# A fused four-stage image network on one core: half-height transposes for half of each attention block, and the residual one block later

## The chip, the cores and the metric

The kernel runs on one core of one Trainium2 chip. The metric is the device time of one execution in microseconds, from three runs; one further execution was profiled. A core has five engines that run side by side: TensorE (PE in the rows, its weight loads PEld), VectorE (DVE), ScalarE (ACT), GpSimd (POOL) and SyncE (SP), which issues the transfers. Each takes its own instructions in order; between engines they wait for each other by semaphores.

## The reference

Four layers are computed one after the other on an input of 4 batch elements, 32 channels and 96 x 96 pixels, all in float32: halo attention, a deformable convolution, a Fourier layer and an FFT convolution. The change touches the attention alone:

```python
BLOCK, HALO, HEADS = (8, 3, 4)
WIN = BLOCK + 2 * HALO
sim = jnp.einsum('bid,bjd->bij', q, k)      # 64 queries x 196 keys, 8 channels per head
attn = jax.nn.softmax(sim, axis=-1)
out = jnp.einsum('bij,bjd->bid', attn, v)
```

The image is cut into 12 x 12 = 144 blocks of 8 x 8 pixels. The 64 queries of a block look at the 14 x 14 = 196 pixels around it, for 4 heads and 4 batch elements.

## The kernel before

`program` (L2120) calls one stage after the other; `stage_attention` (L138) is the first. After the projections it walks over the 144 blocks (`w` in the code), and each engine has a loop of its own in which `step(w, ...)` does pieces of different blocks. This order is written out by hand, and nothing else sets it.

What is computed for a block, by the helper that does it:

- `keys` and `spread` (GpSimd) add the relative position to the keys of a block and spread its queries over the heads.
- `scores(w, p)` (L428, TensorE): `p` is a pair of batch elements. Four products of 32 rows give the scores, 128 rows (2 heads x 64 queries) x 196 keys each, in the PSUM tile `at_sc` of the pair. There is one such tile per pair.
- `maxes(w, p)` (L356, VectorE): negated row maxima, `at_nmx`.
- `exps(w, p)` (L407, ScalarE): four exponentials into `at_probs`, each with its sum.
- `inverse(w, p)` (L361, VectorE): reciprocals of the sums; `norm(w, p)` (L338, GpSimd) multiplies the probabilities by them.
- `transposed(w, b)` (L440, TensorE): for one batch element, four transposes of 128 queries x 98 keys, into PSUM `at_pt[b % 2]`, so pt0 for the elements 0 and 2 and pt1 for 1 and 3. There are two such tiles in all.
- `evac`: VectorE (L365) copies pt0, ScalarE (L401) copies pt1, to `at_pts`, each twice a block.
- `weigh(w)` (L450, TensorE): eight products of transposed probabilities and values, two halves of the keys (`c`) for four batch elements (`b`), into PSUM `at_ov[w % 2]`.
- `residual(w)` (L371, VectorE): four operations, one per head, that add the result to `x_sb`.

TensorE's step `w` (L463) is: transposes of elements 0 and 1 of block w; scores of pair 0 of block w + 2; `weigh` of block w - 1; transposes of elements 2 and 3 of block w; scores of pair 1 of block w + 2. Each set of four transposes waits for the normalised probabilities and for the copy of the PSUM tile that it writes, from the set before. ScalarE's step (L415) is: exponentials of pair 1 of block w + 1, copy, exponentials of pair 0 of block w + 2, copy. VectorE's step is at L383, GpSimd's at L343. A float32 product is two MATMUL records in the trace, a transpose one.

## Time and profile before

| | us |
|---|---|
| median of three runs | 2141.68 (2127.19 to 2234.55) |
| profiled execution, its time | 2117.36 |
| its span in the trace | 2115.6 |
| busy: PE / DVE / ACT / POOL | 1883.8 / 1280.4 / 1129.5 / 737.5 |
| transposes `at_pt`, 2304 matmuls, busy | 311.3 |
| scores `at_sc`, 2304 matmuls, busy | 272.1 |
| product with the values `at_ov`, 2304 matmuls, busy | 155.0 |
| exponentials and the reading of their sums, ACT, 1152 each, busy | 473.8 and 235.3 |
| copies of `at_pt`, 288 each, busy | DVE 196.2, ACT 171.9 |
| maxima `at_nmx`, DVE, 288, busy | 277.7 |

Times are of one profiled execution. A group is named by its line in the kernel, its engine, and the tile that it writes; "idle" is the time for which the engine did nothing just before an instruction, with the instruction that ended it. Matmuls are pipelined, so their records overlap.

### The profile page before, as it was taken

The page shows a single profiled execution, that of the slowest core. Times are in us where ns is not written, and L with a number is a line of the kernel's source. Part 1 is how long each engine was busy: PE and PEld are TensorE (multiplying, and loading weights), DVE is VectorE, ACT ScalarE, POOL GpSimd, SP SyncE. Part 2 cuts the span into 40 slices and gives each one's busy share as a digit, 9 for nine tenths or more (in the row PEclk, how much of TensorE's full clock was granted, in tenths as well). Part 3 has the DMA queues.
Part 4 walks back from the last instruction along what each step waited for, and adds up shares of the span by engine and source line. Part 5 has one row for each costly group of instructions (what it writes and reads, how often), then busy time and mean ns, then how long its engine had stood idle before and what let it go on. Part 6 is the DMA issues. An engine that isn't in the chain of part 4 may idle for free. (4 is left out here: it accounts for less than half of the span.)

```text
span 2115.6 us, 60272 instructions
## 1 busy us (share of the span) xinstructions
PE 1883.8 (89%) x22133; PEld 1312.7 (62%) x22133; DVE 1280.4 (61%) x2688; ACT 1129.5 (53%) x3617; POOL 737.5 (35%) x671
## 2 busy tenths in 40 slices
PE   5699999999999998279999999768757999999999
PEld 3566666666666666045556655467735777777776
DVE  5178888888888888356788888652462222222222
ACT  2378888888888887266777778400121111111111
POOL 0078787887878876122323333000000000000000
PEclk9889999999999999578999999955778999999999
DMA  4401000000000000565676665250002211121110
GB/s 166 135 19 29 27 28 23 27 28 26 25 26 27 26 25 16 141 164 159 185 186 190 185 191 160 52 98 5 16 15 58 65 46 36 36 62 47 36 36 16
DMA packets 164175, 150.05 MB, mean 71 GB/s; under 512 B 60070, under 2 KB 151340, under 8 KB 163935
## 3 DMA queue, kind: packets, MB, share of 16 engines
q1 hardware_dynamic: 164014, 147.88, 26.3%
q8 instruction: 104, 1.70, 0.3%
q14 instruction: 57, 0.46, 0.1%
HBM read 83.18 MB, written 45.89 MB: 61 GB/s over the span
## 5 line engine op out<-in xcount | busy, mean ns | idle before, releaser
L412 ACT ACTIVATE at_probs<-at_sc,at_nmx 128x196 f32<-128x196 f32 x1152 | 473.8, 424 | 114.1 <-DVE at_nmx L358 114.0
L340 POOL TENSOR_TENSOR at_probs<-at_probs,at_rs 128x784 f32<-128x784 f32 x288 | 430.5, 1495 | 152.6 <-DVE at_rs L363 152.5
L358 DVE TENSOR_REDUCE at_nmx<-at_sc 128x4 f32<-128x784 f32 x288 | 277.7, 964 | 122.3 <-PE at_sc L436 122.3
L447 PE MATMUL at_pt<-at_ident,at_probs 128*98 128x128 f32 x2304 | 311.3, 278 | 40.7 <-DVE at_pts L368 40.1
L447 PEld LDWEIGHTS at_pt<-at_ident,at_probs 128*98 128x98 f32 x2304 | 241.0, 128 | 141.5 <-POOL at_probs L340 78.9
L436 PE MATMUL at_sc<-at_kw,at_qw 32*128 32x196 f32 x2304 | 272.1, 355 | 12.0 <-POOL at_qw L329 8.0
L1247 ACT ACTIVATE dn_mix<-dn_mps 128x432 f32<-128x432 f32 x384 | 182.4, 528 | 119.6 <-PE dn_mps L1142 116.3
L2022 PE MATMUL fc_qps<-fc_wk,fc_xs 99*128 99x128 f32 x1728 | 211.0, 279 | 31.3 <-DMA fc_xs<-in_ones 31.3
L412 ACT ACTIVATION_READ_ACCUMULATOR at_probs<-at_sc,at_nmx 128x1 f32 x1152 | 235.3, 204 | 0.0
L2022 PEld LDWEIGHTS fc_qps<-fc_wk,fc_xs 99*128 99x128 f32 x1728 | 202.1, 194 | 42.0 <-issue 39.1
L436 PEld LDWEIGHTS at_sc<-at_kw,at_qw 32*128 32x128 f32 x2304 | 184.3, 187 | 65.3 <-issue 54.8
L1335 DVE TENSOR_SCALAR dn_mix<-dn_mps 128x432 f32<-128x432 f32 x384 | 213.4, 597 | 18.2 <-PE dn_mps L1142 18.2
L368 DVE COPY at_pts<-at_pt 98x512 f32<-98x512 f32 x288 | 196.2, 681 | 0.8 <-PE at_pt L447 0.8
L1155 PEld LDWEIGHTS dn_sps<-dn_mix,dn_patch 128*32 128x32 f32 x6144 | 142.7, 111 | 76.8 <-issue 59.7
L379 DVE SCALAR_TENSOR_TENSOR x_sb<-at_ov,at_hm,x_sb 128x64 f32 (+1 forms) x576 | 163.5, 284 | 27.7 <-PE at_ov L459 2.8
L1142 PE MATMUL dn_mps<-dn_stack,dn_selw 42*128 42x432 f16 x768 | 177.6, 349 | 1.3 <-DVE dn_mix L1335 0.6
L404 ACT COPY at_pts<-at_pt 98x512 f32<-98x512 f32 x288 | 171.9, 597 | 4.5 <-PE at_pt L447 4.5
L1155 PE MATMUL dn_sps<-dn_mix,dn_patch 128*32 128x96 f32 x6144 | 168.5, 249 | 4.1 <-issue 2.8
L1342 DVE COPY dn_sampled<-dn_sps 128x432 f32<-128x432 f32 x192 | 116.6, 607 | 88.0 <-PE dn_sps L1157 81.2
L1934 ACT COPY fc_vsb<-fc_vps 128x384 f32<-128x384 f32 x48 | 23.0, 479 | 267.1 <-PE fc_vps L2033 267.1
L1928 ACT COPY fc_spec<-fc_fps 128x1024 f32<-128x1024 f32 x72 | 73.0, 1014 | 166.5 <-PE fc_fps L2044 166.5
L459 PE MATMUL at_ov<-at_pts,at_vs 98*32 98x256 f32 x2304 | 155.0, 387 | 1.0 <-DVE at_pts L368 1.0
(154 smaller groups left out, 2309.3 us busy)
## 6 DMA issues: line engine op xcount, KB each, us to landing
fc_xs<-fc_xp SPq DMA_DIRECT2D x144, 120.0 KB
dn_slab<-near_image SPq DMA_DIRECT2D x72, 200.0 KB, 4.3
at_vs<-attention_values SPq DMA_DIRECT2D x288, 49.0 KB
dn_offs<-near_maps SPq DMA_DIRECT2D x24, 486.0 KB
near_corners<-dn_split SPq DMA_DIRECT2D x24, 486.0 KB
dn_stack<-near_corners SPq DMA_DIRECT2D x24, 486.0 KB
dn_patch<-near_pixels SPq DMA_DIRECT2D x24, 384.0 KB
attention_values<-ap_vrow SPq DMA_DIRECT2D x21, 256.0 KB, 2.3
```

Source lines behind the costliest of these rows:

```text
L340: nc.gpsimd.tensor_tensor(probs[s][p][:, :, :, :], probs[s][p][:, :, :, :], rs[s][:, 2 * p:2 * p + 2, :].unsqueeze(3).broadcast_to([P, 2, ...
L358: nc.vector.tensor_reduce(nmx[s][:, 2 * p:2 * p + 2, :], sc[p][:, :, 0:2 * NK].rearrange("p b (j k) -> p b j k", j=2), AX.X, ALU.max, nega ...
L368: nc.vector.tensor_copy(pts[s][b][:, :, :, :], pt[b % 2][0:HK, :].rearrange("p (c j q) -> p c j q", c=2, j=2)).then_inc(even_ready, 1)
L404: nc.scalar.copy(pts[s][b][:, :, :, :], pt[b % 2][0:HK, :].rearrange("p (c j q) -> p c j q", c=2, j=2)).then_inc(odd_ready, 1)
L412: nc.scalar.activation(probs[s][p][:, b, j, :], sc[p][:, b, NK * j:NK * j + NK], ACT.Exp, bias=nmx[s][:, 2 * p + b, j:j + 1], accum_out=su ...
L436: mm = nc.tensor.matmul(sc[p][:, b, NK * j:NK * j + NK], qw[s][r, 2 * j:2 * j + 2, :], kw[s][r, :], start=True, stop=True)
L447: mm = nc.tensor.transpose(pt[b % 2][0:HK, o:o + P], probs[s][p][:, b % 2, j, HK * c:HK * c + HK], ident[:, :])
L1142: nc.tensor.matmul(mps[b][:, 0:COLS], selw[:, :], stack[t % 2][:, b, :, :, 4 * k:4 * k + 4], start=True, stop=True).then_inc(mix_done, 1)
L1155: nc.tensor.matmul(sps[C * g:C * g + C, 2 * PX * b:2 * PX * b + 2 * PX], patch[t % 2][:, k, C * b:C * b + C], fours[:, :, g, :], start=Tru ...
L1247: nc.scalar.activation(mix[s % 2][b][:, :], mps[b][:, 0:COLS], ACT.Relu).then_inc(mix_act, 1)
L1335: nc.vector.tensor_scalar(mix[s % 2][b][:, :], mps[b][:, 0:COLS], 0.0, None, ALU.max).then_inc(mix_dve, 1)
L2022: mm = nc.tensor.matmul(qps[m][:, P * b:P * b + P], rows(i, b, dy * W + P * j, P), wk[:, dy, 0:2 * HID], start=(dy == 0), stop=(dy == 2))
```

## The change

Three things change in `stage_attention`.

The transposes of a block are now made pair by pair. The first pair (`p == 0`) is transposed in eight whole transposes as before. The second pair is transposed in 16 of 64 queries each: rows 0 to 63 go to pt0, rows 64 to 127 to pt1. The copies of the second pair therefore write every other run of 64 in `at_pts`, which has one tile per pair now. `pt_ready` counts pairs.

The waits of the transposes stand in `may_transpose`, for both PSUM tiles and the normalised probabilities. `weigh` is split into its two halves of the keys, one behind each set of scores; `may_transpose` of the transposes that come next is called ahead of the last of the four products of each half.

The residual of a block is added one step later, and there is one more step at the end.

```diff
--- before.py
+++ after.py
@@ -260,7 +260,7 @@
             sums = [sbc(f"sums{i}", [P, B, 2]) for i in range(2)]
             rs = [sbc(f"rs{i}", [P, B, 2]) for i in range(2)]
             probs = [[sbc(f"probs{i}_{p}", [P, 2, 2, NK]) for p in range(2)] for i in range(2)]
-            pts = [[sbc(f"pts{i}_{b}", [HK, 2, 2, P]) for b in range(B)] for i in range(2)]
+            pts = [[sbc(f"pts{i}_{p}", [HK, 2, 2, 2, 2, Q64]) for p in range(2)] for i in range(2)]
             sc = [ctx.enter_context(nc.psum_tensor(f"at_sc{p}", [P, 2, 512], F)) for p in range(2)]
             pt = [ctx.enter_context(nc.psum_tensor(f"at_pt{i}", [P, 512], F)) for i in range(2)]
             ov = [ctx.enter_context(nc.psum_tensor(f"at_ov{i}", [P, 512], F)) for i in range(2)]
@@ -286,6 +286,7 @@
                 for x in range(NROW):
                     step((NROW - 1) * NROW + x, NROW - 1, x)
                 step(NWIN, NROW - 1, NROW)
+                step(NWIN + 1, NROW - 1, NROW + 1)
 
             def corner(gy, x):
 
@@ -362,11 +363,14 @@
                     wait(dve, exp_done, w, 4 * 2, 4 * p + 4)
                     nc.vector.reciprocal(rs[s][:, 2 * p:2 * p + 2, :], sums[s][:, 2 * p:2 * p + 2, :]).then_inc(inv_ready, 1)
 
-                def evac(w, b, s):
-                    wait(dve, pt_ready, w, B, b + 1)
+                def evac(w, p, s):
+                    wait(dve, pt_ready, w, 2, p + 1)
                     wait(dve, pv_done, w, 1, -1)
-                    nc.vector.tensor_copy(pts[s][b][:, :, :, :],
-                                          pt[b % 2][0:HK, :].rearrange("p (c j q) -> p c j q", c=2, j=2)).then_inc(even_ready, 1)
+                    if p == 0:
+                        part = pts[s][p][:, 0, :, :, :, :].rearrange("p c j h q -> p (c j h) q")
+                    else:
+                        part = pts[s][p][:, :, :, :, 0, :].rearrange("p b c j q -> p (b c j) q")
+                    nc.vector.tensor_copy(part, pt[0][0:HK, :].rearrange("p (n q) -> p n q", q=Q64)).then_inc(even_ready, 1)
 
                 def residual(w, gy, x):
                     y0, x0 = corner(gy, x)
@@ -387,10 +391,10 @@
                         maxes(w + 2, 0, x % 2)
                     if there(w + 1):
                         inverse(w + 1, 1, (x + 1) % 2)
-                    if there(w + (-1)):
-                        residual(w + (-1), gy, x - 1)
+                    if there(w + (-2)):
+                        residual(w + (-2), gy, x - 2)
                     if there(w):
-                        evac(w, 2, x % 2)
+                        evac(w, 1, x % 2)
                     if there(w + 2):
                         inverse(w + 2, 0, x % 2)
                         maxes(w + 2, 1, x % 2)
@@ -398,15 +402,18 @@
 
             @block.scalar
             def _(act):
-                def evac(w, b, s):
-                    wait(act, pt_ready, w, B, b + 1)
+                def evac(w, p, s):
+                    wait(act, pt_ready, w, 2, p + 1)
                     wait(act, pv_done, w, 1, -1)
-                    nc.scalar.copy(pts[s][b][:, :, :, :],
-                                   pt[b % 2][0:HK, :].rearrange("p (c j q) -> p c j q", c=2, j=2)).then_inc(odd_ready, 1)
+                    if p == 0:
+                        part = pts[s][p][:, 1, :, :, :, :].rearrange("p c j h q -> p (c j h) q")
+                    else:
+                        part = pts[s][p][:, :, :, :, 1, :].rearrange("p b c j q -> p (b c j) q")
+                    nc.scalar.copy(part, pt[1][0:HK, :].rearrange("p (n q) -> p n q", q=Q64)).then_inc(odd_ready, 1)
 
                 def exps(w, p, s):
                     wait(act, max_ready, w, 2, p + 1)
-                    wait(act, pt_ready, w, B, 2 * p + 2 - 2 * B)
+                    wait(act, pt_ready, w, 2, p + 1 - 2 * 2)
                     for b in range(2):
                         for j in range(2):
                             nc.scalar.activation(probs[s][p][:, b, j, :], sc[p][:, b, NK * j:NK * j + NK], ACT.Exp,
@@ -416,11 +423,11 @@
                     if there(w + 1):
                         exps(w + 1, 1, (x + 1) % 2)
                     if there(w):
-                        evac(w, 1, x % 2)
+                        evac(w, 0, x % 2)
                     if there(w + 2):
                         exps(w + 2, 0, x % 2)
                     if there(w):
-                        evac(w, 3, x % 2)
+                        evac(w, 1, x % 2)
                 rows(act, step)
 
             @block.tensor
@@ -437,43 +444,57 @@
                                                   start=True, stop=True)
                     mm.then_inc(scores_ready, 1)
 
-                def transposed(w, b, s):
-                    p = b // 2
+                def may_transpose(w, p):
                     wait(pe, normed, w, 2, p + 1)
-                    wait(pe, (even_ready, odd_ready)[b % 2], w, 2, p)
-                    for c in range(2):
-                        for j in range(2):
-                            o = (2 * c + j) * P
-                            mm = nc.tensor.transpose(pt[b % 2][0:HK, o:o + P], probs[s][p][:, b % 2, j, HK * c:HK * c + HK], ident[:, :])
+                    wait(pe, even_ready, w, 2, p)
+                    wait(pe, odd_ready, w, 2, p)
+
+                def transposed(w, p, s):
+                    for b in range(2):
+                        for c in range(2):
+                            for j in range(2):
+                                if p == 0:
+                                    o = P * (2 * c + j)
+                                    mm = nc.tensor.transpose(pt[b][0:HK, o:o + P], probs[s][p][:, b, j, HK * c:HK * c + HK], ident[:, :])
+                                for h in range(2 * p):
+                                    o, r = Q64 * (4 * b + 2 * c + j), slice(Q64 * h, Q64 * h + Q64)
+                                    mm = nc.tensor.transpose(pt[h][0:HK, o:o + Q64], probs[s][p][r, b, j, HK * c:HK * c + HK], ident[r, r])
                     mm.then_inc(pt_ready, 1)
 
-                def weigh(w, g, i):
+                def weigh(w, g, i, c, following):
 
                     s = i % 2
-                    wait(pe, even_ready, w, 2, 2)
-                    wait(pe, odd_ready, w, 2, 2)
-                    wait(pe, v_loaded[s], g, 16 * VSRING, 32 * (i // 2 + 1))
-                    wait(pe, res_step, w, HEADS, -HEADS)
-                    for c in range(2):
-                        for b in range(B):
-                            mm = nc.tensor.matmul(ov[s][C * b:C * b + C, 0:256], vs[i % VSRING][:, c, C * b:C * b + C],
-                                                  pts[s][b][:, c, :, :], start=(c == 0), stop=(c == 1))
-                    mm.then_inc(pv_done, 1)
+                    if c == 0:
+                        wait(pe, even_ready, w, 2, 2)
+                        wait(pe, odd_ready, w, 2, 2)
+                        wait(pe, v_loaded[s], g, 16 * VSRING, 32 * (i // 2 + 1))
+                        wait(pe, res_step, w, HEADS, -HEADS)
+                    for b in range(B):
+                        if b == B - 1 and following is not None:
+                            may_transpose(*following)
+                        mm = nc.tensor.matmul(ov[s][C * b:C * b + C, 0:256], vs[i % VSRING][:, c, C * b:C * b + C],
+                                              pts[s][b // 2][:, b % 2, c, :, :, :].rearrange("p j h q -> p (j h q)"), start=(c == 0), stop=(c == 1))
+                    if c == 1:
+                        mm.then_inc(pv_done, 1)
 
                 def step(w, g, i):
                     s = i % 2
                     if there(w):
+                        if not there(w + (-2)):
+                            may_transpose(w, 0)
                         transposed(w, 0, s)
-                        transposed(w, 1, s)
                     if there(w + 2):
                         scores(w + 2, 0, s)
                     if there(w + (-1)):
-                        weigh(w + (-1), g, i - 1)
+                        weigh(w + (-1), g, i - 1, 0, (w, 1) if there(w) else None)
+                    elif there(w):
+                        may_transpose(w, 1)
                     if there(w):
-                        transposed(w, 2, s)
-                        transposed(w, 3, s)
+                        transposed(w, 1, s)
                     if there(w + 2):
                         scores(w + 2, 1, s)
+                    if there(w + (-1)):
+                        weigh(w + (-1), g, i - 1, 1, (w + 1, 0) if there(w + 1) else None)
                 for w in range(-2, 2 * VSRING):
                     step(w, w // VSRING, w % VSRING)
                 with pe.Fori(2, NWIN // VSRING - 1) as g:
```

On TensorE, in the middle of the loop (numbers are of buffers; `at_probs1_0` is the first pair of an odd block): scores of a second pair, transposes of a first pair, scores of the next first pair, and the product with the values. Before:

```order
L436 MATMUL at_sc1<-at_kw0,at_qw0 128x196 [waits at_exp_done]
L436 MATMUL at_sc1<-at_kw0,at_qw0 128x196 x3
L447 MATMUL at_pt0<-at_ident,at_probs1_0 98x128 [waits at_even_ready,at_normed]
L447 MATMUL at_pt0<-at_ident,at_probs1_0 98x128 x3
L447 MATMUL at_pt1<-at_ident,at_probs1_0 98x128 [waits at_odd_ready,at_normed]
L447 MATMUL at_pt1<-at_ident,at_probs1_0 98x128 x3
L436 MATMUL at_sc0<-at_kw1,at_qw1 128x196 [waits at_exp_done,at_keys_ready]
L436 MATMUL at_sc0<-at_kw1,at_qw1 128x196 x3
L459 MATMUL at_ov0<-at_pts0_0,at_vs0 32x256 [waits at_v_loaded0,at_res_step,at_odd_ready,at_even_ready]
L459 MATMUL at_ov0<-at_pts0_1,at_vs0 32x256
L459 MATMUL at_ov0<-at_pts0_2,at_vs0 32x256
L459 MATMUL at_ov0<-at_pts0_3,at_vs0 32x256
```

Now, from the second half of the product with the values on:

```order
L475 MATMUL at_ov1<-at_pts1_0,at_vs3 32x256 x2
L475 MATMUL at_ov1<-at_pts1_1,at_vs3 32x256
L475 MATMUL at_ov1<-at_pts1_1,at_vs3 32x256 [waits at_odd_ready,at_even_ready,at_normed]
L458 MATMUL at_pt0<-at_ident,at_probs1_0 98x128 x4
L458 MATMUL at_pt1<-at_ident,at_probs1_0 98x128 x4
L443 MATMUL at_sc0<-at_kw1,at_qw1 128x196 [waits at_exp_done,at_keys_ready]
L443 MATMUL at_sc0<-at_kw1,at_qw1 128x196 x3
L475 MATMUL at_ov0<-at_pts0_0,at_vs0 32x256 [waits at_v_loaded0,at_res_step,at_odd_ready,at_even_ready]
L475 MATMUL at_ov0<-at_pts0_0,at_vs0 32x256
L475 MATMUL at_ov0<-at_pts0_1,at_vs0 32x256
L475 MATMUL at_ov0<-at_pts0_1,at_vs0 32x256 [waits at_odd_ready,at_even_ready,at_normed]
```

The transposes of a first pair had a wait for each PSUM tile ahead of each four of them; now one wait for both tiles stands ahead of the matmul before them. The product with the values stood in one piece behind the scores of a first pair and now has a half there and a half ahead of the whole transposes.

On ScalarE, one and a half steps at the same place. Before:

```order
L404 COPY at_pts0_1<-at_pt1 98x512 [waits at_pv_done,at_pt_ready]
L412 ACTIVATE at_probs0_0,at_sums0<-at_sc0,at_nmx0 128x196 [waits at_pt_ready,at_max_ready]
L412 ACTIVATE at_probs0_0,at_sums0<-at_sc0,at_nmx0 128x196 x3
L404 COPY at_pts0_3<-at_pt1 98x512 [waits at_pv_done,at_pt_ready]
L412 ACTIVATE at_probs0_1,at_sums0<-at_sc1,at_nmx0 128x196 [waits at_pt_ready,at_max_ready]
L412 ACTIVATE at_probs0_1,at_sums0<-at_sc1,at_nmx0 128x196 x3
L404 COPY at_pts1_1<-at_pt1 98x512 [waits at_pv_done,at_pt_ready]
```

Now:

```order
L412 COPY at_pts0_0<-at_pt1 98x512 [waits at_pv_done,at_pt_ready]
L419 ACTIVATE at_probs0_0,at_sums0<-at_sc0,at_nmx0 128x196 [waits at_pt_ready,at_max_ready]
L419 ACTIVATE at_probs0_0,at_sums0<-at_sc0,at_nmx0 128x196 x3
L412 COPY at_pts0_1<-at_pt1 98x8x64 [waits at_pv_done,at_pt_ready]
L419 ACTIVATE at_probs0_1,at_sums0<-at_sc1,at_nmx0 128x196 [waits at_pt_ready,at_max_ready]
L419 ACTIVATE at_probs0_1,at_sums0<-at_sc1,at_nmx0 128x196 x3
L412 COPY at_pts1_0<-at_pt1 98x512 [waits at_pv_done,at_pt_ready]
```

Nothing moved: a copy of pt1 stands behind each four exponentials, the copy of a second pair (`at_pts0_1`, formerly `at_pts0_3`) behind the exponentials of a first pair. Its shape is 8 runs of 64.

On VectorE, one step. Before:

```order
L368 COPY at_pts1_0<-at_pt0 98x512 [waits at_pv_done,at_pt_ready]
L358 TENSOR_REDUCE at_nmx1<-at_sc0 128x4 [waits at_scores_ready]
L363 RECIPROCAL at_rs0<-at_sums0 128x4 [waits at_exp_done]
L379 SCALAR_TENSOR_TENSOR x_sb<-at_ov0,at_hm,x_sb 128x8x8 [waits at_pv_done]
L379 SCALAR_TENSOR_TENSOR x_sb<-at_ov0,at_hm,x_sb 128x8x8 [waits at_res_step] x3
L368 COPY at_pts1_2<-at_pt0 98x512 [waits at_pv_done,at_pt_ready]
L363 RECIPROCAL at_rs1<-at_sums1 128x4 [waits at_exp_done]
L358 TENSOR_REDUCE at_nmx1<-at_sc1 128x4 [waits at_scores_ready]
```

Now:

```order
L373 COPY at_pts1_0<-at_pt0 98x512 [waits at_pv_done,at_pt_ready]
L359 TENSOR_REDUCE at_nmx1<-at_sc0 128x4 [waits at_scores_ready]
L364 RECIPROCAL at_rs0<-at_sums0 128x4 [waits at_exp_done]
L383 SCALAR_TENSOR_TENSOR x_sb<-at_ov1,at_hm,x_sb 128x8x8 [waits at_pv_done]
L383 SCALAR_TENSOR_TENSOR x_sb<-at_ov1,at_hm,x_sb 128x8x8 [waits at_res_step] x3
L373 COPY at_pts1_1<-at_pt0 98x8x64 [waits at_pv_done,at_pt_ready]
L364 RECIPROCAL at_rs1<-at_sums1 128x4 [waits at_exp_done]
L359 TENSOR_REDUCE at_nmx1<-at_sc1 128x4 [waits at_scores_ready]
```

The order is the same too; the residual reads the other `at_ov` tile, that of the block before.

## Rows read from the trace of the kernel before

**Rows 1.** The page: PE's granted clock in tenths, 40 slices of 52.9 us.
```profile
PEclk9889999999999999578999999955778999999999
```

**Rows 2.** Busy time by stretch: us, busy of each engine, granted clock, DMA.
```profile
400.00:500.00 100.00, 94.02 (x947) 65.42 (x940) 85.69 (x199) 85.71 (x356) 79.79 (x79) 1.00 0.09 27
```

**Rows 3.** Waits, 200 to 800 us: who waited for whom, us, times, longest.
```profile
ACT at_probs L412 <- DVE at_nmx L358: 87.5, 118, 0.8
...
PE at_pt L447 <- DVE at_pts L368: 34.8, 118, 0.3
```

**Rows 4.** Instructions in time order, one block: start, us, engine, line [idle before].
```profile
405.83 1.08 PE L447 MATMUL at_pt<-at_ident,at_probs 128*98 128x128 f32 x8
...
406.03 0.42 ACT L412 ACTIVATE at_probs<-at_sc,at_nmx 128x196 f32<-128x196 f32 x1
406.08 1.24 DVE L379 SCALAR_TENSOR_TENSOR x_sb<-at_ov,at_hm,x_sb 128x64 f32 x4
406.08 1.50 POOL L340 TENSOR_TENSOR at_probs<-at_probs,at_rs 128x784 f32<-128x784 f32 x1 [1.01 <-DVE at_rs L363]
...
406.84 0.93 PE L436 MATMUL at_sc<-at_kw,at_qw 32*128 32x196 f32 x8
...
407.24 0.68 DVE L368 COPY at_pts<-at_pt 98x512 f32<-98x512 f32 x1
...
407.55 0.21 ACT L412 ACTIVATION_READ_ACCUMULATOR at_probs<-at_sc,at_nmx 128x1 f32 x1
407.65 0.60 ACT L404 COPY at_pts<-at_pt 98x512 f32<-98x512 f32 x1
407.84 0.17 DVE L363 RECIPROCAL at_rs<-at_sums 128x4 f32<-128x4 f32 x1
407.92 0.95 DVE L358 TENSOR_REDUCE at_nmx<-at_sc 128x4 f32<-128x784 f32 x1
408.03 0.83 PEld L447 LDWEIGHTS at_pt<-at_ident,at_probs 128*98 128x98 f32 x8 [0.56 <-POOL at_probs L340]
408.06 1.05 PE L447 MATMUL at_pt<-at_ident,at_probs 128*98 128x128 f32 x8 [0.29 <-DVE at_pts L368]
...
408.98 0.42 ACT L412 ACTIVATE at_probs<-at_sc,at_nmx 128x196 f32<-128x196 f32 x1 [0.74 <-DVE at_nmx L358]
...
409.05 0.93 PE L436 MATMUL at_sc<-at_kw,at_qw 32*128 32x196 f32 x8
...
409.91 1.07 PE L459 MATMUL at_ov<-at_pts,at_vs 98*32 98x256 f32 x16
410.03 0.97 DVE L358 TENSOR_REDUCE at_nmx<-at_sc 128x4 f32<-128x784 f32 x1 [0.56 <-PE at_sc L436]
...
410.60 0.59 ACT L404 COPY at_pts<-at_pt 98x512 f32<-98x512 f32 x1
...
410.91 0.53 PE L447 MATMUL at_pt<-at_ident,at_probs 128*98 128x128 f32 x3
...
411.12 0.42 ACT L412 ACTIVATE at_probs<-at_sc,at_nmx 128x196 f32<-128x196 f32 x1
```

**Rows 5.** Records of two lines: count, ns min/median/max, first and last start.
```profile
L447 PE MATMUL at_pt<-at_ident,at_probs x2304: 272/273/450, 109.0 to 841.8; 128*98 128x128 f32 x192
...
L459 PE MATMUL at_ov<-at_pts,at_vs x2304: 379/379/635, 119.5 to 843.7; 98*32 98x256 f32 x192
```

**Rows 6.** In order of time, the last stage, PE and its weight loads.
```profile
1913.55 1.09 PE L2044 MATMUL fc_fps<-fc_qk,fc_dft 64*64 64x256 f32 x16
...
1914.57 0.97 PEld L2055 LDWEIGHTS fc_ips<-fc_dft,fc_prod 128*128 128x128 f32 x8 [0.39 <-issue]
```

**Rows 7.** In order of time, PE near the start of the stage.
```profile
119.45 1.94 PE L459 MATMUL at_ov<-at_pts,at_vs 98*32 98x256 f32 x16
121.32 1.94 PE L447 MATMUL at_pt<-at_ident,at_probs 128*98 128x128 f32 x8
123.19 0.60 PE L436 MATMUL at_sc<-at_kw,at_qw 32*128 32x196 f32 x4
```

## The prediction

> **What bounds the kernel now.** I read the page first, for where attention lies and at which clock; then busy time by stretch; then the waits of 200 to 800 us; and last the instructions of one block of queries in order of time. Attention lies in slices 3 to 16 of 40, at the full clock but for its start [rows 1]. There TensorE (PE) is busy 94.02 of 100 us at a granted clock of 1.00 [rows 2], so it looks like the bound. The waits say otherwise: in every block PE stands still once for VectorE's (DVE) copy of the transposed probabilities, 34.8 us over 118 blocks, and ScalarE (ACT) stands still once for DVE's maxima, 87.5 us [rows 3]. So the block is timed by rings of dependences that close after one block. Names in what follows: T1 and T2 are the transposes of a block's first and second pair, S1 and S2 the score products, O the product with the values, X1 and X2 the four exponentials of a pair, M1 and M2 the maxima, E the DVE copies, A the ACT copies.
>
> The period is 5.09 us: X1 starts at 406.03 and again at 411.12 [rows 4]. The transposes run from 109.0 to 841.8 us, 16 to a block [rows 5], so 144 blocks at 5.1.
>
> Ring 1, PE and DVE, binds today. T1 starts at 408.06, T2 at 410.91 (2.85, with S1 and O between); the residual starts 0.25 after T2 (405.83 to 406.08), since it waits for O; the copy E starts 1.16 after it (407.24); T1 follows 0.82 later, after 0.29 of idle time put down to that copy [rows 4]. 2.85 + 0.25 + 1.16 + 0.82 = 5.08.
>
> Ring 2, ACT and DVE, is just as long. X1 406.03, reciprocal 407.84 (1.81), M2 407.92 (0.08), X2 408.98 (1.06), ACT's copy 410.60 (1.62), next X1 411.12 (0.52): 5.09 [rows 4]. Its only slack is that the reciprocal starts 0.08 after the last read of X1's sums ends (407.55 + 0.21), and some of that is signalling. **So with ring 1 gone the period can fall to 5.01 at the lowest**, and the change leaves every member of ring 2 in its place: in ACT's order a copy stands between the exponentials as before, and on DVE the reciprocal still stands ahead of M2.
>
> **The change part by part.** *Residual a block later.* The same four operations in the same place, but their input is long complete: ring 1 loses its 0.25 and opens. One more residual stands alone at the end: +1 us once.
>
> *Whole transposes of the first pair.* Eight, as before: 1.01 from the first to the next product (405.83 to 406.84). What changes is who must be out of the way. Before, the first four wrote pt0 and waited for DVE alone, the other four wrote pt1 and waited for ACT. Now one wait for both stands ahead of all eight, and one matmul earlier still: before the last of four matmuls of the product with the values, whose split halves stand behind S1 and S2.
>
> *Half transposes of the second pair.* 16 of 64 columns instead of 8 of 128. The trace has no transpose on a row group. Lower bound: products on two row groups do run side by side. The score products, 32 rows each, issue eight in 0.93 [rows 4]; the 64-row products of the last stage issue 16 of 256 columns in 1.09 [rows 6]. A whole transpose takes (1.08 - 0.27) / 7 = 0.115 [rows 4, 5], near 0.11 without the lead-in; a pair of halves would take half of it, 8 x 0.055 = 0.44, and with the lead-in (1.01 - 8 x 0.11 = 0.13) T2 is 0.57. Upper bound: the loads go one by one and set the pace. Loads of 128 columns, with only 64 moving, come every (0.97 - 0.19) / 7 = 0.11 [rows 6]; scaled to 98 columns that is 0.085, times 16 plus 0.13 is 1.5. I take 0.57, since the rows on row groups are nearer in kind.
>
> *Product with the values in two halves.* As many instructions; one more lead-in, about 0.31, on PE, which has idle time for it below.
>
> *Copies.* Two on each engine, 512 elements as before; those of the second pair are written in runs of 64. I take the same 0.68 and 0.60 [rows 4]. PE's own work falls to about 1.01 + 0.86 + 0.55 + 0.57 + 0.86 + 0.55 = 4.4 us.
>
> *The new wait.* ACT's order is X2, A1, X1, A2. The second copy A2 cannot start until the four exponentials X1 of two blocks ahead are through. T1 of the next block, all of it, now waits for A2; S1 stands behind T1 on PE; M1 waits for S1; the next X1 waits for M1. That is ring 3, closed after one block:
> - X1 to A2: 1.62 (406.03 to 407.65)
> - A2 itself: 0.60
> - end of a copy to PE's first matmul after it: 0.14 (DVE's ends at 407.24 + 0.68 = 407.92, PE starts at 408.06)
> - the held matmul, two passes: the 16 records take 1.07, one takes 0.38 [rows 4, 5], so a pass is (1.07 - 0.38) / 3 = 0.23
> - last pass to the first transpose: 410.91 - 409.91 - 0.69 = 0.31
> - T1: 1.01
> - S1 to M1: 0.98 (409.05 to 410.03)
> - M1 to X1: 1.06 (407.92 to 408.98)
>
> Sum 5.95 us. Before, only the second half of T1 waited for ACT, and no product was held: 1.62 + 0.60 + 0.14 + 0.57 (1.01 less four transposes of 0.11) + 0.98 + 1.06 = 4.97, hidden under 5.09. Ring 4 is the same through the second pair (X2, A1, held matmul, T2, S2, M2): 4.94 + T2, so 5.51 with 0.57; it takes over above 1.01. DVE's work, 5.09 less its idle 0.56, is 4.5 and fits. GpSimd is no member: it normalises a second pair from 406.08 to 407.58, for the T2 at 410.91; that the row of loads at 408.03 names it means only that its semaphore stands in the same wait [rows 4].
>
> So the period goes from 5.09 to 5.95. Over 142 repeats 0.86 x 142 = +122 us, +1 for the last residual: the profiled execution's 2117.4 becomes 2240. The median of the runs shown is 24.3 above that execution, so I put the forecast at **2265 us**. PE's idle time for DVE goes; ACT's for the maxima grows, and PE's for ACT's copy appears.
>
> **The rivals.**
> *The cover works, no slower (0.07).* The wait for ACT is not what holds T1. For it: of PE's idle time at the transposes the trace puts nothing in this stretch down to ACT's copy [rows 3]. Against it: A2 would have to end 0.86 earlier, and ACT takes its work in order. Then ring 2 rules: 5.01, 0.08 x 142 = -11 us: 2131 (or no change at all).
> *PE is the bound, faster (0.03).* Rings 2 and 3 are both misread and the block takes PE's 4.4 us: -98 us, about 2044. The trace itself speaks against it: ring 2 closes to 0.01.
> *Half transposes bound by their loads (0.04).* T2 = 1.5 makes ring 4 6.44 us: 1.35 x 142 = +192, 2335 us. It decides from T2 = 1.01. The Trainium skill ("TensorE: Matmul & The Clock Gate", on LDWEIGHTS) says that a load's time goes by its columns and not by its rows, about columns / 1.2 in ns; 16 loads of 98 would by that page be an estimated 1.31 us, so the halved rows buy nothing. By that rule, too, the change makes the weight side dearer; the eight loads of 98 columns in 0.83 us here [rows 4] are paced by their matmuls and can't tell.
> *The clock falls (0.04).* At the start of the stage the trace shows the clock's lower level (1.2 GHz): T1 to S1 takes 1.87 (121.32 to 123.19) and O takes 1.87 (119.45 to 121.32) [rows 7]. If PE's new idle time, 1.5 us in 5.95, kept it there, ring 3 would be at most 1.62 + 0.60 + 0.14 + 2 x 0.54 + 1.87 + 2 x 0.98 + 1.06 = 8.3: 3.2 x 142 = +454, about 2596 us. Against it: PE never rests over a microsecond, and the clock stays at 1.00 from 200 to 800 us [rows 1, 2]. The skill's same page (Part 4) says that transposes don't count as activity for the clock in the way that products do; then what counts, the same products per block, would be spread over 5.95 us instead of 5.09. No row here tells the two apart.
>
> **How the numbers follow.** The forecast has 0.82, the rivals the rest. Its own range: without the held matmul's pass (0.23) and from the lowest run rather than the median, 2222; with T2 at 1.2, or 0.25 more in the signals, 2300. That leaves out the rivals, 0.18, and little more, so the range is 2222 to 2300. About 2% is what a measurement of this kernel tells from no change. Faster 0.03, same 0.07, slower 0.90.
>
> **What would show it.** Right: in the steady stretch X1 repeats every 5.9 to 6.0 us; ACT's copy is what PE waits for ahead of L475, about 0.6 us a block, and DVE's copy no longer; L458 x8 takes 1.0, L461 x16 about 0.6; ACT's idle time for the maxima grows from 0.74 to about 1.6 a block, in two places; clock 1.00. Wrong: a period at or under 5.1, PE's wait put down to GpSimd or DVE, L461 above 1.0, or a clock below 1.00 in the stretch.

## The result, and the profile after

| | before | changed |
|---|---|---|
| median of the runs, us | 2134.43 (2101.45 to 2234.55, 4 runs) | 2247.33 (2231.12 to 2273.68, 4 runs) |
| ratio, with 95% interval | | 1.060 (1.041 to 1.079) |
| span of the profiled execution | 2115.6 | 2248.9 |
| up to the first transpose | 109.0 | 108.6 |
| attention, first to last transpose | 732.8 | 880.0 |
| from there to the end | 1273.8 | 1260.2 |
| period of a block, steady stretch | 5.086 | 5.950 |

The change makes the kernel slower by 6%. The ratio, here and below, compares the fast runs of each kernel (2 of 4 before, 3 of 4 changed; an execution more than 1.5% above its kernel's fastest is left out), while the medians are of all runs. All of the added time lies in attention, +147.2 us in the profiled executions; the stages behind, which it does not touch, happen to be 13.6 us shorter. "Period" here and below is the median distance between the first exponentials of successive blocks, over blocks 40 to 120 of a trace.

The page of the changed kernel: TensorE's (PE's) clock in slices of 56.2 us, and the groups of instructions that answer to those of the prediction (busy and mean, then the idle time just before them and its releaser).

```profile
PEclk9855999999999999985799999997686999999999
...
L419 ACT ACTIVATE at_probs<-at_sc,at_nmx 128x196 f32<-128x196 f32 x1152 | 472.6, 422 | 248.0 <-DVE at_nmx L359 248.0
...
L475 PE MATMUL at_ov<-at_pts,at_vs 98*32 98x256 f32 x2304 | 335.7, 408 | 53.9 <-ACT at_pts L412 53.2
...
L373 DVE COPY at_pts<-at_pt 98x512 f32<-98x512 f32 x288 | 197.5, 686 | 178.8 <-PE at_pt L458 177.2
```

ScalarE (ACT) waits 248 us for the maxima; PE waits 53.2 us for ACT's copy, at the product with the values, where `may_transpose` now stands. The copies themselves, 686 and 596 ns, cost what they did, runs of 64 or not. In the steady stretch the waits are (who waited for whom, 220 to 850 us: us, times, longest):

```profile
ACT at_probs L419 <- DVE at_nmx L359: 162.7, 212, 0.8
DVE at_pts L373 <- PE at_pt L458: 123.2, 106, 1.3
...
PE at_ov L475 <- ACT at_pts L412: 42.1, 105, 0.4
```

These answer to [rows 3]: ACT waited for the maxima once a block and now waits twice (212 times in 106 blocks); PE's wait for the copy of VectorE (DVE) is gone, and a wait for ACT's stands in its place, 0.40 a block. One block in order of time (start, duration, engine, line, [idle before]), which answers to [rows 4]:

```profile
401.60 0.43 ACT L419 ACTIVATE at_probs<-at_sc,at_nmx 128x196 f32<-128x196 f32 x1 [0.79 <-DVE at_nmx L359]
...
403.21 0.60 ACT L412 COPY at_pts<-at_pt 98x512 f32<-98x512 f32 x1
...
403.95 0.59 PE L475 MATMUL at_ov<-at_pts,at_vs 98*32 98x256 f32 x2 [0.40 <-ACT at_pts L412]
...
404.48 1.08 PE L458 MATMUL at_pt<-at_ident,at_probs 128*98 128x128 f32 x8
404.55 0.43 ACT L419 ACTIVATE at_probs<-at_sc,at_nmx 128x196 f32<-128x196 f32 x1 [0.74 <-DVE at_nmx L359]
...
405.49 0.93 PE L443 MATMUL at_sc<-at_kw,at_qw 32*128 32x196 f32 x8
...
406.16 0.60 ACT L412 COPY at_pts<-at_pt 98x512 f32<-98x512 f32 x1
...
406.46 0.97 DVE L359 TENSOR_REDUCE at_nmx<-at_sc 128x4 f32<-128x784 f32 x1 [0.18 <-PE at_sc L443]
...
407.43 0.65 PE L461 MATMUL at_pt<-at_ident,at_probs 64*98 64x64 f32 x16
...
407.55 0.42 ACT L419 ACTIVATE at_probs<-at_sc,at_nmx 128x196 f32<-128x196 f32 x1 [0.79 <-DVE at_nmx L359]
...
408.01 0.93 PE L443 MATMUL at_sc<-at_kw,at_qw 32*128 32x196 f32 x8
```

Ring 3 of the prediction can be read off: X1 401.60, A2 403.21 (1.61), its end 403.81 (0.60), the held matmul 403.95 (0.14), T1 404.48 (0.53), S1 405.49 (1.01), M1 406.46 (0.97), X1 again 407.55 (1.09). The sum is 5.95, with nothing left over, and over blocks 40 to 119 the medians of the same members add up to 5.95 too.

The clock explains the remainder of the 147 us. Two stretches of attention (length; busy time of PE, its weight loads, DVE, ACT and GpSimd, with the number of instructions; granted clock; DMA):

```profile
125.00:209.00 84.00, 84.00 (x580) 52.16 (x578) 46.13 (x102) 46.40 (x185) 40.72 (x40) 0.50 0.07 19
215.00:960.00 745.00, 694.22 (x7017) 398.31 (x7016) 555.98 (x1252) 552.67 (x2253) 509.18 (x500) 1.00 0.08 22
```

At the start of attention PE runs at the lower level, 1.2 GHz, for 119.5 us (95.5 to 215.0); before it was 27.3 us (95.9 to 123.2, [rows 7] lie in it). A block takes 8.13 there instead of 5.95. So 0.864 x 142 = 123 us of the 147 are the longer ring, and about 24 are some 11 to 12 blocks at 2.2 us more each. From 215 us on the clock is 1.00.

### The profile page after: what moved, and what is told of

It reads as the page before. It is cut to its first block and busy times, and to the rows that moved or that the text cites. A ratio compares the mean times of both kernels' runs of the same rounds, so it can differ in the third digit from the quotient of the medians.

```text
span 2248.9 us, 62165 instructions
## 1 busy us (share of the span) xinstructions
PE 2003.0 (89%) x23285; PEld 1290.1 (57%) x23285; DVE 1293.7 (58%) x2688; ACT 1141.1 (51%) x3617; POOL 736.7 (33%) x671
## 3 DMA queue, kind: packets, MB, share of 16 engines
q1 hardware_dynamic: 164014, 147.88, 24.7%
## 5 line engine op out<-in xcount | busy, mean ns | idle before, releaser
L475 PE MATMUL at_ov<-at_pts,at_vs 98*32 98x256 f32 x2304 | 335.7, 408 | 53.9 <-ACT at_pts L412 53.2
L443 PE MATMUL at_sc<-at_kw,at_qw 32*128 32x196 f32 x2304 | 289.2, 373 | 11.8 <-POOL at_qw L330 7.8
L443 PEld LDWEIGHTS at_sc<-at_kw,at_qw 32*128 32x128 f32 x2304 | 196.4, 198 | 52.6 <-ACT at_probs L419 26.5
L475 PEld LDWEIGHTS at_ov<-at_pts,at_vs 98*32 98x32 f32 x2304 | 81.0, 110 | 232.4 <-issue 120.0
L458 PE MATMUL at_pt<-at_ident,at_probs 128*98 128x128 f32 x1152 | 167.5, 292 | 0.7 <-ACT at_pts L412 0.7
L383 DVE SCALAR_TENSOR_TENSOR x_sb<-at_ov,at_hm,x_sb 128x64 f32 (+1 forms) x576 | 159.0, 276 | 15.5
L458 PEld LDWEIGHTS at_pt<-at_ident,at_probs 128*98 128x98 f32 x1152 | 128.3, 134 | 65.6 <-issue 63.6
```

The costliest lines, as they stand in the source:

```text
L443: mm = nc.tensor.matmul(sc[p][:, b, NK * j:NK * j + NK], qw[s][r, 2 * j:2 * j + 2, :], kw[s][r, :], start=True, stop=True)
L458: mm = nc.tensor.transpose(pt[b][0:HK, o:o + P], probs[s][p][:, b, j, HK * c:HK * c + HK], ident[:, :])
L475: mm = nc.tensor.matmul(ov[s][C * b:C * b + C, 0:256], vs[i % VSRING][:, c, C * b:C * b + C], pts[s][b // 2][:, b % 2, c, :, :, :].rearran ...
```

## The experiments

Three questions. Is it ring 3, closed through ACT's copy, that sets the period, and which part of the change closes it? What did the old period consist of, and what are the change's parts worth by themselves? And what of the clock? Each kernel's profile gives a period, a length of attention and a low-clock stretch at its start:

| run | period | attention | low clock at its start | to the end | median of runs | ratio to before |
|---|---|---|---|---|---|---|
| before | 5.086 | 732.8 | 27.3 | 1273.8 | | |
| changed | 5.950 | 880.0 | 119.5 | 1260.2 | 2247.33 (4) | 1.060 |
| changed, again | 5.954 | 864.5 | 61.4 | 1262.4 | 2238.48 (1) | |
| e1_t1_late | 5.526 | 825.2 | 119.5 | 1283.9 | 2178.59 (4) | 1.036 (1.023 to 1.050) |
| e2_whole | 5.955 | 868.5 | 61.4 | 1299.8 | 2254.82 (4) | 1.063 (1.037 to 1.090) |
| e3_whole_split | 5.150 | 762.8 | 75.1 | 1299.2 | 2147.61 (4) | |
| b1_residual | 5.062 | 729.7 | 27.3 | 1270.9 | 2106.35 (10) | 0.997 (0.990 to 1.003) |
| b2_maxima | 5.086 | 736.7 | 34.1 | 1255.3 | 2100.47 (8) | 0.992 (0.987 to 0.997) |
| b3_both | 4.977 | 723.2 | 34.1 | 1271.8 | 2098.0 (10) | 0.999 (0.994 to 1.003) |
| e4_whole_scores_first | 4.883 | 703.3 | 23.9 | 1268.2 | 2091.53 (4) | |
| e4_again | 4.883 | 703.3 | 23.9 | 1268.1 | 2102.06 (12) | 0.998 (0.992 to 1.003) |
| e5_half_scores_first | 4.703 | 678.1 | 23.9 | 1303.4 | 2098.2 (4) | |
| c1_filled | 5.954 | 855.3 | 20.4 | 1303.9 | 2257.91 (4) | 1.062 (1.050 to 1.074) |
| c2_half_filled | 4.703 | 678.0 | 17.0 | 1303.2 | 2093.51 (6) | |

The experiments were run in three groups, on two chips, with the kernel before beside them at 2128.05 (e1 to e4), 2115.41 (b1 to b3, e5, the other chip) and 2104.92 (the others). Each ratio is to the kernel before of the same group; where none stands, none was determined. Each profile is of a single execution. The last stages vary by up to 49 us from profile to profile although no kernel changes them, so the mechanism is judged by the period, and the whole time only where it is said.

**1. Release T1's wait later.** The gate of the first pair moves from ahead of the last matmul of the product to right ahead of the transposes. Ring 3 loses its held matmul; ring 4, through the second pair, keeps it.

```diff
@@ changed kernel, TensorE's step
-                        if not there(w + (-2)):
-                            may_transpose(w, 0)
+                        may_transpose(w, 0)
                         transposed(w, 0, s)
...
-                        weigh(w + (-1), g, i - 1, 1, (w + 1, 0) if there(w + 1) else None)
+                        weigh(w + (-1), g, i - 1, 1, None)
```

> The changed kernel with one edit: the wait of the whole transposes (T1) stands right ahead of them, no longer ahead of the last product with the values. Ring theory: the held matmul's 0.23 and the 0.31 behind it leave ring 3, which becomes 1.62 + 0.60 + 0.14 + 1.01 + 0.98 + 1.06 = 5.41. The second pair's wait is left where it is, so ring 4 (4.94 + T2, and T2 is 0.58 in the profile after) now sets the period: 5.52. Span about 0.43 x 142 = 61 us under the changed kernel's. Rival (the one wait for both copies costs the time, wherever it stands): the period stays at 5.95. Rival (PE's mode changes and the split of the product cost the time): it stays at 5.95 too.

Measured: 5.526. One block of it in order of time:

```profile
502.31 0.42 ACT L419 ACTIVATE at_probs<-at_sc,at_nmx 128x196 f32<-128x196 f32 x1 [0.88 <-DVE at_nmx L359]
...
503.92 0.60 ACT L412 COPY at_pts<-at_pt 98x512 f32<-98x512 f32 x1
...
504.66 0.59 PE L475 MATMUL at_ov<-at_pts,at_vs 98*32 98x256 f32 x2 [0.48 <-ACT at_pts L412]
...
505.18 0.65 PE L461 MATMUL at_pt<-at_ident,at_probs 64*98 64x64 f32 x16
...
505.76 0.93 PE L443 MATMUL at_sc<-at_kw,at_qw 32*128 32x196 f32 x8
...
506.74 0.98 DVE L359 TENSOR_REDUCE at_nmx<-at_sc 128x4 f32<-128x784 f32 x1
```

This is ring 4: X2 502.31, A1 503.92 (1.61), its end (0.60) and signal (0.14), held matmul to T2 0.52, T2 to S2 0.58, S2 to M2 0.98, and 1.10 to the next X2: 5.53. PE now waits for ACT once a block at the second pair. One wait, put behind the held matmul instead of ahead of it, took 0.42 from the period. The ratio goes from 1.060 to 1.036 (the two intervals overlap; the period is the firm number). The prediction's ring 4 (5.51) took over where it was said to.

**2. Whole transposes for the second pair too,** all else as changed. If the half transposes were the bound, or worth their name here, the period would move.

```diff
@@ changed kernel, transposed(w, p, s); the copies of both pairs take the form of the first
-                                if p == 0:
+                                if True:
                                     o = P * (2 * c + j)
...
-                                for h in range(2 * p):
+                                for h in range(0):
```

> The changed kernel with the second pair in eight whole transposes again; all waits, the split product and the late residual are left. Ring theory: T2 goes from 0.58 to 1.01, ring 4 from 5.52 to 5.95, ring 3 stays at 5.95: the period does not move, 5.95, and the span is within 5 us of the changed kernel's at the same clock. Rival (the half transposes and their mode change are what costs): the period falls back towards 5.1. Rival (PE's work is the bound): it grows by 0.43 to 6.4, +61 us.

Measured: 5.955, the changed kernel's period. In order of time:

```profile
499.95 0.42 ACT L413 ACTIVATE at_probs<-at_sc,at_nmx 128x196 f32<-128x196 f32 x1 [1.28 <-DVE at_nmx L359]
...
501.56 0.59 ACT L406 COPY at_pts<-at_pt 98x512 f32<-98x512 f32 x1
...
502.30 0.59 PE L469 MATMUL at_ov<-at_pts,at_vs 98*32 98x256 f32 x2 [0.46 <-ACT at_pts L406]
...
505.90 0.42 ACT L413 ACTIVATE at_probs<-at_sc,at_nmx 128x196 f32<-128x196 f32 x1 [1.28 <-DVE at_nmx L359]
```

The transposes of the second pair take about 1.01 instead of 0.58 and the block takes the same 5.95: their 0.43 lay in slack, and just filled it (ring 4 is then 4.94 + 1.01 = 5.95, as long as ring 3). So in the change as it was made the half transposes neither cost nor gained.

**3. Take both gates away too:** whole transposes, the waits ahead of the transposes, and ACT's copy awaited only by the four transposes that write its tile. What stays of the change is the product in two halves, one signal for the eight transposes of a pair, and the residual a block later.

```diff
@@ on top of experiment 2
                 def may_transpose(w, p):
                     wait(pe, normed, w, 2, p + 1)
                     wait(pe, even_ready, w, 2, p)
-                    wait(pe, odd_ready, w, 2, p)
 
                 def transposed(w, p, s):
                     for b in range(2):
+                        if b == 1:
+                            wait(pe, odd_ready, w, 2, p)
...
-                        if b == B - 1 and following is not None:
-                            may_transpose(*following)
```

> Both pairs in whole transposes, each four with a wait for the one copy that they need, right ahead of them, as in the kernel before; what is left of the change is the product with the values in two halves and the residual a block later. Ring theory: ring 3 is back at 4.97 and ring 1 stays open, so ring 2 rules: a period of 5.01 to 5.16, span from 11 us under to 10 us over the kernel before. Rival (the split product or the late residual costs the time): a period near 5.9.

Measured: 5.150. Of the 0.86 that the change added, 0.80 is gone, and this run differs from experiment 2 in the waits alone: it is the waits that cost the time, by where they stand and by asking for both copies at once. What is left over the kernel before is 0.06. With the residual late and all else as before the period is 5.062 (experiment 4), so the split product and the one signal per pair together cost 0.09.

The value lies in the expected range, but not for the expected reason: ring 2 does not set it. From X2's copy on, in order of time:

```profile
502.48 0.60 ACT L406 COPY at_pts<-at_pt 98x512 f32<-98x512 f32 x1
...
503.13 0.40 PEld L453 LDWEIGHTS at_pt<-at_ident,at_probs 128*98 128x98 f32 x4 [0.36 <-ACT at_pts L406]
...
503.71 0.93 PE L437 MATMUL at_sc<-at_kw,at_qw 32*128 32x196 f32 x8
...
504.57 0.64 PE L468 MATMUL at_ov<-at_pts,at_vs 98*32 98x256 f32 x8
...
505.14 1.08 PE L453 MATMUL at_pt<-at_ident,at_probs 128*98 128x128 f32 x8
```

Here the second half of T2 waits for the copy A1, and S2, a half of the product, T1 and the next S1 stand behind it on PE. The ring that closes is one over two blocks (medians of blocks 40 to 119): S1 to M1 0.98, to X1 1.09, to the reciprocal 1.77, to M2 0.10, to X2 1.09, to A1 1.61, A1 itself 0.60, from its end to S2 0.63, to the half product 0.86, to T1 0.57, to S1 1.01. The sum is 10.30 us, twice 5.15. The half product between S2 and T1 is a member of it.

**4. The old rings.** The kernel before with the residual a block later alone (b1); with the second maxima ahead of the first reciprocal alone, which opens ring 2 (b2); with both (b3). b1 and b3 also have the one more step at the end.

```diff
@@ kernel before, VectorE's step (b3_both has both)
-                    if there(w + (-1)):
-                        residual(w + (-1), gy, x - 1)
+                    if there(w + (-2)):
+                        residual(w + (-2), gy, x - 2)
...
-                        inverse(w + 2, 0, x % 2)
                         maxes(w + 2, 1, x % 2)
+                        inverse(w + 2, 0, x % 2)
```

> The kernel before with one edit: the residual a block later (and one more step at the end). Ring theory: ring 1 opens, ring 2 (X1, reciprocal, M2, X2, ACT's copy) is untouched and takes over at once: a period of 5.01 to 5.06 instead of 5.09, 4 to 11 us of the span. Rival (the idle time that the trace puts down to DVE's copy, 0.29 a block, is what a block can gain): 4.79, 42 us.

> The kernel before with one edit: on VectorE the maxima of the second pair (M2) stand ahead of the reciprocal of the first pair's sums. Ring theory: ring 2 is cut, ring 1 is not: the period stays at 5.08 to 5.09. Rival (ring 2 alone binds and ring 1 is a story): it falls towards 4.97.

> The kernel before with both edits: residual a block later and M2 ahead of the reciprocal. Ring theory: rings 1 and 2 are both cut, and what is left is ring 3 as it was before the change (1.62 + 0.60 + 0.14 + 0.57 + 0.98 + 1.06 = 4.97): a period of 4.97 to 5.0, about 13 to 17 us of the span, more than the two edits bring by themselves. Rival (the gains only add up): 5.05 or more, under 6 us.

Measured: 5.062, 5.086, 4.977. Their waits over 200 to 750 us, b1 first, then b2, then b3:

```profile
ACT at_probs L413 <- DVE at_nmx L359: 81.0, 109, 0.7
PE at_pt L448 <- DVE at_pts L369: 2.0, 9, 0.2
```

```profile
ACT at_probs L412 <- DVE at_nmx L358: 72.8, 108, 0.7
PE at_pt L447 <- DVE at_pts L368: 32.3, 108, 0.3
```

```profile
ACT at_probs L413 <- DVE at_nmx L359: 72.1, 110, 0.7
PE at_pt L448 <- DVE at_pts L369: 1.9, 9, 0.2
```

The late residual takes away PE's wait, 32 to 2 us (the kernel before has 32.2 in the same window), and almost nothing of the period, 0.02: ring 2 is there at once. Opening ring 2 alone gives nothing, since ring 1 holds. Both together give 0.11, down to ring 3 in its old form, for which the prediction's sum is 4.97. The waits above don't show that ring, because the second half of T1 is delayed by under 0.1 us, but the members do: in b3 the medians are X1 to A2 1.61, A2 0.61, its end to S1 0.69, S1 to M1 0.98, M1 to X1 1.09, together 4.98. Both gains were forecast a little too high: b1's period is at the upper edge of its range (5.06), and b3's attention is 9.6 us shorter, not 13 to 17. Three rings within 0.12 of each other: a wait that ends in every block is no proof that taking it away gains anything. In the whole time these are 0 to 1%; b2's interval (0.987 to 0.997) lies below 1 although its attention is not shorter, and a ratio this near to 1 is not to be read as the edit's.

**5. A version meant to beat both.** Scores go ahead of the transposes in each half of PE's step, so T1 and S1 no longer stand in one chain behind ACT's copy; DVE's order is put to match. e4 has whole transposes; e5 has halves for the second pair, with one whole transpose ahead that carries the waits and whose result is overwritten.

```diff
@@ on top of experiment 3: TensorE's step
+                    if there(w + 2):
+                        scores(w + 2, 0, s)
                     if there(w):
                         may_transpose(w, 0)
                         transposed(w, 0, s)
-                    if there(w + 2):
-                        scores(w + 2, 0, s)
...
+                    if there(w + 2):
+                        scores(w + 2, 1, s)
@@ VectorE's step: maxes(w+2, 0), inverse(w+1, 1), evac(w, 0), residual(w-2),
@@ maxes(w+2, 1), inverse(w+2, 0), evac(w, 1)
@@ e5, in transposed, on top of that
+                    if p == 1:
+                        nc.tensor.transpose(pt[0][0:HK, 0:P], probs[s][p][:, 0, 0, 0:HK], ident[:, :])
```

> As the run with whole transposes and a wait per copy, and with another order: on TensorE the scores of a pair (two blocks ahead) stand ahead of the transposes of a pair, and on VectorE the maxima stand first, ahead of the copy (M1, reciprocal, E1, residual, M2, reciprocal, E2). Ring theory: rings 2 and 3 are both cut, since the scores no longer stand behind the transposes that wait for ACT's copy, and M2 no longer behind the reciprocal of X1. Left are PE's own work (before: 5.09 less 0.30 idle, and one more lead-in of 0.1) and the order of DVE: a period of 4.85 to 4.95, so 20 to 35 us under the kernel before. Rival (the period is a floor of PE or DVE near 5.05 whatever the order): no gain, within 5 us of the kernel before.

> As the run with the scores first (which gave a period of 4.88), but with the second pair in half transposes; their waits are carried by one whole transpose more, into the same place, ahead of them. On TensorE this takes 1.01 down to 0.58 plus about 0.25 for the added one: 0.83. Theory that in that order PE's own work is the bound: the period falls by up to 0.18, to 4.70 to 4.80. Theory that DVE and the signals bound it: it stays at 4.88.

Measured: 4.883 and 4.703. Busy time from 400 to 500 us and one half block of e4 (its second execution) in order of time:

```profile
400.00:500.00 100.00, 100.00 (x988) 66.29 (x984) 87.89 (x206) 91.03 (x370) 84.34 (x82) 1.00 0.09 27
```

```profile
500.40 0.93 PE L437 MATMUL at_sc<-at_kw,at_qw 32*128 32x196 f32 x8
...
501.26 1.08 PE L453 MATMUL at_pt<-at_ident,at_probs 128*98 128x128 f32 x8
...
502.27 0.64 PE L468 MATMUL at_ov<-at_pts,at_vs 98*32 98x256 f32 x8
...
502.84 0.93 PE L437 MATMUL at_sc<-at_kw,at_qw 32*128 32x196 f32 x8
```

Here PE is the bound at last: 100.00 of 100.00 us busy, and 0.86 + 1.01 + 0.57 = 2.44 to a half block, twice 2.44 a period. Only now are half transposes worth something. e5, at the second pair:

```profile
503.01 0.93 PE L443 MATMUL at_sc<-at_kw,at_qw 32*128 32x196 f32 x8
...
503.87 0.32 PE L455 MATMUL at_pt<-at_ident,at_probs 128*98 128x128 f32 x1
504.12 0.65 PE L466 MATMUL at_pt<-at_ident,at_probs 64*98 64x64 f32 x16
...
504.70 0.64 PE L478 MATMUL at_ov<-at_pts,at_vs 98*32 98x256 f32 x8
...
505.27 0.93 PE L443 MATMUL at_sc<-at_kw,at_qw 32*128 32x196 f32 x8
```

The halves take 0.58 where whole ones take 1.01, and the transpose ahead takes 0.25 of that back: 0.18 a block, 25.2 us of attention (703.3 to 678.1). PE is busy 99.92 of 100 us there too (400 to 500). No run has the waits on the half transposes themselves.

e4 was run once more, for more executions.

> The run with whole transposes and the scores first once more, for its time: a period of 4.88 and, from the 0.20 a block that it is under the kernel before, a median 25 to 40 us under it (ratio 0.981 to 0.988).

Its attention is 703.3 both times, 29.5 us shorter than before. Its whole time is not measurably shorter: 0.998 (0.992 to 1.003), a median 2.9 us under that of the kernel before where 25 to 40 were expected. What stands against the gain is the clock of the whole run. Over the 50 runs of the kernel before in the three groups (mean clocks of 0.914 to 0.950), time goes with PE's mean granted clock: 2.16 us less for 0.001 more, with a scatter of 4.8 us about that line. The mean distance of a kernel's runs from the line is its time at equal clock:

| | mean clock | from the line of before, us | change of period x 142 |
|---|---|---|---|
| changed | 0.928 | +120 | +123 |
| e2_whole | 0.932 | +131 | +123 |
| e1_t1_late | 0.927 | +53 | +62 |
| e3_whole_split | 0.926 | +8 | +9 |
| b1 / b2 / b3 | 0.935 to 0.938 | -5 / -5 / -16 | -3 / 0 / -15 |
| e4, twice | 0.936, 0.927 | -24, -27 | -29 |
| e5_half_scores_first | 0.911 | -58 | -54 |
| c1_filled | 0.935 | +138 | +123 |
| c2_half_filled | 0.924 | -52 | -54 |

At equal clock each kernel stands where its period puts it, to 9 us (c1 to 15, which stays unexplained). Closer than some 8 us this is not to be read: 120 us more at the full clock raise the mean clock by 0.004 by themselves, and e5's and c2's runs (0.875 to 0.941 and 0.902 to 0.957) go beyond the clocks on which the line rests. But e5's runs, and e4's the second time, had a lower mean clock than the 0.934 and 0.937 of the kernel before beside them, and that costs what they gain. Whether denser work in attention brings this on in the stages behind is open: at the low level there e5's and c2's profiles show 319 and 312 us, but e4's 226 and 236, before's 254, and of the kernels with longer periods the changed one's 227 and 219, e1's 274, e3's 291, e2's 302 and c1's 312. So I have a version whose attention is 30 to 55 us shorter, but none that is measured to be faster than the kernel before.

**6. The clock at the start.** The changed kernel once more; then with five products of 512 columns added in PE's idle time ahead of the first blocks (they write a PSUM tile that is overwritten), and the same five in e5.

```diff
@@ changed kernel (c1) and e5 (c2), TensorE
+                def fill(n):
+                    for _ in range(n):
+                        nc.tensor.matmul(pt[0][:, :], ident[:, :], pixels[:, 0:512], start=True, stop=True)
...
+                    if w < 0:
+                        fill(2)
                     step(w, w // VSRING, w % VSRING)
+                    if w == -1:
+                        fill(1)
```

> The changed kernel once more, for where the low clock lies. In the first profile the stage began at the lower clock and stayed there for 119.5 us (27.3 in the kernel before), with a period of 8.13 us. If that length belongs to the kernel, it is near 119 again; if it is chance, it comes out anywhere from 27 to 120. The period at the full clock is 5.95 by either.

> The changed kernel with five products of 512 columns more on TensorE at the start of the stage, into a transpose tile that is overwritten afterwards: two ahead of the scores of blocks 0 and of 1 each, one behind those of block 1. They fill TensorE's idle time while the first exponentials are waited for. If the low clock comes from that idle start, it ends earlier: by about 110 us of the profile instead of 215, and the attention is some 20 to 30 us shorter at the same period of 5.95. If the block's own pattern at the low clock keeps it there, the stretch is as long as before, and the span is 0 to 3 us longer for the added products.

> Half transposes with the scores first (period 4.70) and the five products at the start. Period 4.70. If the start holds the clock down, the low stretch in attention (23.9 us without them) is gone or shorter, and the span is 55 to 65 us under the kernel before's at an equal rest. If the half transposes themselves cost clock, the granted clock from 130 us on is under 1.00 in places, and the time scatters as it did without the added products (2047 to 2185).

Measured: the same kernel's low stretch was 61.4 us the second time, not 119.5, with the same 5.954 after it; attention 864.5, which is 15.5 less. With the products, 20.4 us in three pieces, and the clock is up for good at 127.3. The start of attention in c1 (31 us, granted clock 0.68), and in the changed kernel's second execution:

```profile
96.00:127.00 31.00, 25.00 (x145) 15.32 (x146) 11.22 (x19) 16.72 (x68) 16.59 (x18) 0.68 0.09 27
```

```profile
97.00:159.00 62.00, 53.53 (x360) 34.96 (x360) 29.34 (x59) 34.98 (x141) 32.88 (x34) 0.51 0.08 24
```

With the added work the stretch was shorter than in either execution without it, and attention is 855.3 from its first transpose on, 24.7 and 9.2 us under those two; the added products themselves put that first transpose at 110.6 instead of 108.6 and 109.7. This is one execution, and the low clock ended at 127.3, not near 110. The kernel as a whole is not measurably faster: 1.062 against before. In e5, where the stretch was short already, 23.9 became 17.0 and attention stayed at 678 us. c2's six runs still scatter, from 2017.36 to 2130.74, although the clock was 1.00 from 120 us to the end of attention in its profile; the 312 us at the low level lie behind attention.

How long the stretch is goes with the order of the work on PE. In the five traces of kernels with the split product and the transposes ahead of the scores (changed twice, e1, e2, e3) it is 61 to 120 us; in the four with the old order (before, b1 to b3) 27 to 34; in the three of e4 and e5, scores first, 23.9. So it is a side effect of the change, worth some 9 to 25 us in the changed kernel, and it varies from one execution to the next; it is not the main part of what the change costs. Which part of the order brings it on was not tested.

## Why the prediction was right, point by point

**The period.** 5.95 forecast, 5.950 and 5.954 measured. The terms, as read from the block above: X1 to A2 1.61 (forecast 1.62), the copy 0.60, signal 0.14, held matmul to T1 0.53 (0.54), T1 1.01, S1 to M1 0.97 (0.98), M1 to X1 1.09 (1.06). None was off by more than 0.03. The mechanism is shown by edits too: experiment 1 takes two members out of ring 3 and the next ring sets the period, and experiment 3 takes the late waits away and 0.80 of the 0.86 goes.

**Ring 4, 4.94 + T2.** It does not bind in the changed kernel: there M2 waits in DVE's order for the reciprocal behind X1's sums. Its 5.51 is confirmed by experiment 1, which bares it at 5.526.

**The half transposes.** T2 forecast as 0.57 from the rows of 32- and 64-row products, measured 407.43 to 408.01, 0.58. The rival with loads one by one (T2 = 1.5) is out.

```profile
L461 PE MATMUL at_pt<-at_ident,at_probs x2304: 216/216/343, 112.2 to 988.6; 64*98 64x64 f32 x192
```

Each record lasts 216 ns (the three numbers are minimum, median and maximum), and 16 of them span 0.65 us. In the trace the two halves of a block of 128 rows start within 7 ns of each other, loads and transposes alike, and a pair follows the other every 56 ns; whole transposes start every 109 ns. The Trainium skill ("TensorE: Matmul & The Clock Gate", on LDWEIGHTS), by which 16 loads of 98 columns would be an estimated 1.31 us, does not describe this stretch, which takes 0.58. The Trainium skill's page "TensorEngine Tiling (Array Packing)", Key Properties, says that different tiles can load and multiply in parallel, and the pairs agree with it. That the halves gained nothing in the change is shown by experiment 2, and that they gain 0.18 a block where PE is the bound, by experiment 5; 0.43, without the transpose that carries the waits, was not run.

**Residual a block later.** Forecast: it opens ring 1, and the period could then fall to 5.01 at the lowest. The part by itself gave 5.062, so ring 2's floor was put 0.05 too low. Over blocks 40 to 119, the gap between the last read of X1's sums and the reciprocal went from 0.07 to 0.03 and not to nothing, and the exponentials ahead of it and the steps from the reciprocal to X2 came out 0.07 longer together, A1 to X1 0.05 shorter.

**The waits.** PE's for DVE's copy is gone, ACT's for the maxima is 0.79 + 0.74 in two places (forecast about 1.6), and PE's for ACT's copy is 0.40 a block where I said about 0.6. The time is not affected by that miss, since the ring and not the idle time sets the period.

**PE's own work, 4.4.** The changed kernel can't show it. e5 can, since PE is busy almost without a pause there: 4.70 less the 0.25 of the transpose ahead is 4.45.

**The clock.** Forecast 1.00 in the stretch; it is, from 215 us on. That PE's new idle time would keep the clock down throughout is refuted by 745 us at 1.00. But the term that the sum lacked is here: the sum had nothing for the start of attention, and the low level lasted 119.5 us in one execution and 61.4 in the other, instead of 27.3. By the rows this was worth about 24 and 9 us. The period at the low level, 8.13, is under the 8.3 that the rival had as its most.

**The sum.** 122 + 1 forecast for attention; 147 in the profiled execution, 123 of it the ring. That the total of 2265 comes within 18 us of the median measured is in part luck, since three misses that have nothing to do with the rings partly offset each other. The sum lacked 24 us for the clock at the start. The stages behind came out 14 us shorter, with 27 us less at the low level in them (227 against 254). And 24 us were added for the distance from the profiled execution to the median, which in the changed kernel is 3 us the other way (2250.66 and 2247.33), 28 too much. 24 less 14 less 28 puts the measured median 18 under the forecast. As a ratio, 2265 / 2141.68 is 1.058; the medians measured give 1.053, and the ratio in the first table is 1.060, with an interval (1.041 to 1.079) that holds both. The lower end of the range is also a slip: the lowest run and the shorter ring give 2127.19 + 0.63 x 142 + 1, or 2218, and not 2222.

**The other rivals.** The cover does not work: experiment 1 moves the wait and the period follows by what ring 4 allows. PE was not the bound: in the changed kernel it is busy 694 of 745 us and waits for ACT's copy in every block.
